# Graph attention: the bend of the leaky slope moved from ScalarE to GpSimd

## The chip, the cores and the metric

The kernel runs on one core of one Trainium2 chip. The metric is the device time of one execution in microseconds (us). The engines are named as in the profile: PE (TensorE matmul), PEld (TensorE weight load), DVE (VectorE), ACT (ScalarE), POOL (GpSimd), SP (SyncE, which starts most DMAs).

## The reference, cut to what matters

The whole network has four graph layers and four feed-forward layers over 625 nodes and 10000 edges. The change touches only the first graph layer, a graph attention with 8 heads:

```python
score = s_src + s_dst + einsum(diff, a_dif) + einsum(abs(diff), a_abs) + einsum(hr_src * hr_dst, a_prd)
alpha = jax.nn.leaky_relu(score, negative_slope=0.2)
m = segment_max(alpha.T, src)
ex = exp(alpha.T - m[src])
att = ex / (segment_sum(ex, src)[src] + 1e-16)
out = segment_sum(att * h_e[:, dst], src)
```

## The kernel before

The layer is computed densely: for a tile t of 125 source nodes and a head h there is a score for each of the 625 target nodes, a tile of 125 x 625 float32. There are 5 tiles (NT) and 8 heads (HEADS0), so 40 heads k = 8 t + h in one pipeline. A term u of the source node (the tile U, one number for each partition, tile and head) is left out of the raw score x and comes back in the biases. The leaky slope is split: leaky(x+u) = 0.2 (x+u) + 0.8 relu(x+u), and the exponential is taken of the two parts apart and multiplied. For one head k the engines do the following, each in its own written-out order, tied by semaphores:

- PE `raw(k)`: six matmuls into RAW in PSUM (L923, L925), after `raw_taken` of head k-1.
- DVE `raw_scores(k)`: RAW plus the gathered pair scores TSC into SP0[k % 4], with the row maximum (L2125; its second input TSC lies in SBUF with a stride of 8 elements; counts up raw_taken).
- ACT `bent(k)`: BENT[k % 4] = relu(SP0 + U), 125 x 625 (L1455; bent_ready).
- DVE `shift(k)`: two tiny instructions on SH, 125 x 2 and 125 x 1 (L2134, L2136; negmax_ready), the biases of the two exponentials. L2134 has two SBUF inputs beside its scalar, SLOPES and UP.
- ACT `exp_scores(k)`: two exponentials of 125 x 625, SP0 with scale 0.2 (L1461; slope_ready) and BENT with scale 0.8 (L1462; bend_ready).
- POOL `counted(k)`: SP0 times the edge counts CNT (L1744; counted_ready).
- DVE `weighted(k)`: SP0 times BENT with the row sum (L2144; both inputs in SBUF; weights_summed).
- PE `turn_head(k)`: five transposes (L935); ACT `turned_head(k)`: their copy (L1466); PE: ten matmuls with the values HE (L957).

In iteration k of the loop DVE runs `left` (every fourth head, L2105), raw_scores(k+4), weighted(k+2), shift(k+4), `add_heads` at h == 2 of the next tile (L2152 to L2160 and the norm statistics, L1863 to L1866, L1871), and every third head one group of the weight quantization of the next layer (`quantized`, L2114 and L2115, 128 x 512). ACT runs exp_scores(k+3), turned_head(k+1), bent(k+4), `left` (L1447) and its part of the quantization (L1416, L1417, L1428). POOL runs counted(k+3), an inverse root (L1700) once a tile and `signed`, its part of the quantization (L1738, 128 x 512). SP starts the loads of the pair scores of tile t+1 (L568) when a tile's raw scores have been taken.

Of the kernel before, what the change touches and what calls it, by code (L numbers as in the profile page):

```python
# [19 lines left out]
ALU, ACT, AX = mybir.AluOpType, mybir.ActivationFunctionType, mybir.AxisListType  # L20

N, E, D = 625, 10000, 512
P, NT = 125, 5
# [5 lines left out]
HEADS0, DH0 = 8, 64  # L29
# [3 lines left out]
NEG = -1.0e30  # L33
# [178 lines left out]
def program(nc, a, out, loops):  # L212
# [3 lines left out]
    def sb(name, shape, dt=F32):  # L216
        return ctx.enter_context(nc.sbuf_tensor(name, shape, dt))
# [15 lines left out]
    with ctx:  # L233
# [51 lines left out]
        TS = sb("TS", [128, SCORES_AHEAD, HEADS0])  # L285
        CW = sb("CW", [128, ET, 2])
        NODE = sb("NODE", [P, 2, NT])
        U = sb("U", [P, NT, HEADS0])
        UP = sb("UP", [P, NT, HEADS0, 2])
        SH = sb("SH", [P, 2, HEADS0, 2])  # L290
        SLOPES = sb("SLOPES", [P, 2])
# [23 lines left out]
        def view(at, parts, *shape, dt=F32):  # L315
# [69 lines left out]
        BENT = [view(PT_ + 12250, P, N), BENT_SPARE[:, :]] + [  # L385
            MASK_FLAT[:, 1250 * b:1250 * (b + 1)].bitcast(F32) for b in range(2)]
        SP0 = [view(HT_ + 625 * b, P, N) for b in range(4)]
# [67 lines left out]
        scaled_ready, raw_filled, raw_taken = sem("scaled_ready"), sem("raw_filled"), sem("raw_taken")  # L455
        bent_ready, slope_ready, bend_ready = sem("bent_ready"), sem("slope_ready"), sem("bend_ready")
        counted_ready = sem("counted_ready")
        heads_turned, heads_taken = sem("heads_turned"), sem("heads_taken")
        negmax_ready, exp_ready, sums_ready = sem("negmax_ready"), sem("exp_ready"), sem("sums_ready")
        weights_summed, prob_ready = sem("weights_summed"), sem("prob_ready")  # L460
# [818 lines left out]
        def _(act):  # L1279
            n = Tally("act")  # L1280
            psum = Slots(slots, n)
            fn = nc.scalar.activation
# [39 lines left out]
            s, k, _ = psum.next("N")  # L1322
# [5 lines left out]
            for t in range(NT):  # L1328
                s = take("N")
                fn(HR[0:P, t, :, 0, :], s.ap[0:P, :].rearrange("p (h d) -> p h d", d=DH0), ACT.Copy)  # L1330
                fn(Y[0:P, t, :], s.ap[0:P, :], ACT.Copy).then_inc(s.taken, 1)
            for t in range(NT):
                s = take("N")
                fn(HE[:, t, :], s.ap[0:P, :], ACT.Copy).then_inc(s.taken, 1)
            psum.skip(T=ET // 4, W=STEPS + 1)
            s = take("N")
            fn(U[:, :, :], s.ap[0:P, 0:8 * NT].rearrange("p (t h) -> p t h", t=NT), ACT.Copy)\
                .then_inc(s.taken, 1)
            s = take("N")
            fn(PRODUCT[:, :], s.ap[:, 0:HEADS0], ACT.Copy).then_inc(s.taken, 1)  # L1340
# [54 lines left out]
            for t in range(NT):  # L1395
                for rows in (HRT_LOW, HRT_HIGH):
                    s = take("T")
# [49 lines left out]
                fn(LEFT[:, u % 2, 0, :, :], s.ap[:, 0:4 * P].rearrange("p (h n) -> p h n", h=4), ACT.Copy)\  # L1447
                    .then_inc(scaled_ready, 1)

            def bent(k):  # L1450
                t, h = divmod(k, HEADS0)
                act.wait_ge(raw_taken, k + 1)
                if k >= 4:
                    act.wait_ge(weights_summed, k - 3)
                fn(BENT[k % 4], SP0[k % 4], ACT.Relu, bias=U[:, t, h:h + 1]).then_inc(bent_ready, 1)  # L1455

            def exp_scores(k):
                t, h = divmod(k, HEADS0)
                act.wait_ge(negmax_ready, n.add(negmax_ready))
                act.wait_ge(bent_ready, k + 1)  # L1460
                fn(SP0[k % 4], SP0[k % 4], ACT.Exp, bias=SH[:, t % 2, h, 0:1], scale=0.2).then_inc(slope_ready, 1)  # L1461
                fn(BENT[k % 4], BENT[k % 4], ACT.Exp, bias=SH[:, t % 2, h, 1:2], scale=0.8).then_inc(bend_ready, 1)  # L1462
# [5 lines left out]
            HEADS_ALL = NT * HEADS0  # L1468
            left(0)
            left(1)  # L1470
            for k in range(4):
                bent(k)
                if k:
                    exp_scores(k - 1)
            act.wait_ge(uv_ready, 3)
            ahead = quantized(0, late=True)
            turned_head(0)
            for k in range(HEADS_ALL):
                if k + 3 < HEADS_ALL:
                    exp_scores(k + 3)  # L1480
                if k + 1 < HEADS_ALL:
                    turned_head(k + 1)
                if k + 4 < HEADS_ALL:
                    bent(k + 4)
                if k % 4 == 2:
                    left((k + 6) // 4)
                if k == 2 or (k % 3 == 0 and k):
                    next(ahead, None)
# [192 lines left out]
        def _(pool):  # L1681
# [52 lines left out]
            def signed(u):  # L1734
                for k, (j, c, width) in enumerate(groups_of(u)):
# [3 lines left out]
                     .then_inc(quant_ready, 1)  # L1739
                    yield  # L1740

            def counted(k):
                pool.wait_ge(slope_ready, k + 1)
                g.tensor_tensor(SP0[k % 4], SP0[k % 4], CNT[:, k // HEADS0, :], ALU.mult).then_inc(counted_ready, 1)  # L1744

            pool.wait_ge(sums_merged, NT)
            ahead = signed(0)
            for k in range(3):
                counted(k)
            for k in range(NT * HEADS0):  # L1750
                t, h = divmod(k, HEADS0)
                if k + 3 < NT * HEADS0:
                    counted(k + 3)
                if h == 2 and t:
                    inverse_roots([t - 1])
                if k % 3 == 2 and k >= 5:
                    next(ahead, None)
# [74 lines left out]
        def _(dve):  # L1832
# [10 lines left out]
            def step(ins):  # L1843

                ins.then_inc(vector_step, 1)
                dve.wait_ge(vector_step, n.add(vector_step))
# [239 lines left out]
            v.memset(SLOPES[:, 0:1], -0.2)  # L2086
            v.memset(SLOPES[:, 1:2], -0.8)
            v.memset(UP[:, :, :, 0:1], 0.0)
            step(v.tensor_scalar(UP[:, :, :, 1], U[:, :, :], -0.8, None, ALU.mult))
            for lo in (0, DH0):  # L2090
                rows = slice(lo, lo + DH0)
                v.tensor_tensor(
# [37 lines left out]
            def shift(k):  # L2130
                t, h = divmod(k, HEADS0)
                z = SH[:, t % 2, h, :]
                dve.wait_ge(raw_taken, k + 1)
                step(v.scalar_tensor_tensor(z, SLOPES[:, :], HM[:, t % 2, 0, h:h + 1], UP[:, t, h, :],  # L2134
                                            ALU.mult, ALU.add))
                v.tensor_scalar(z[:, 1:2], z[:, 1:2], 0.0, None, ALU.min).then_inc(negmax_ready, 1)  # L2136
                n.add(negmax_ready)

            def weighted(k):
# [562 lines left out]
```

## Time and profile before

| What | Value |
|---|---|
| median of 3 runs | 2611.85 us (2609.61 to 2612.3) |
| time of the profiled execution | 2604.66 us |
| its span in the profile | 2602.7 us |
| busy share PE / DVE / ACT / POOL | 86% / 42% / 28% / 20% |
| the pipeline of 40 heads | from 478.4 us to about 667 us of the span |

The span is the time from the first to the last instruction in the trace; the execution's own time is 2 us longer. Busy shares are means over the whole network; for the change only the stretch of the 40 heads counts, 7% of the span.

### The profile page before, as it was taken

What the parts mean: (1) busy time and instruction counts of PE and PEld (TensorE: products, weight loads), DVE (VectorE), ACT (ScalarE), POOL (GpSimd) and SP (SyncE); (2) the same over time, 40 slices, a digit from 0 to 9 for tenths busy, and PEclk for the clock granted to TensorE, in tenths of its full rate; (3) what the DMA queues carried; (4) which work ended last, traced back from release to release, by engine and by line L of the source; (5) the groups of instructions that cost most, each with busy time, mean ns of one, the idle gap of its engine ahead of it and who ended that gap; (6) DMA issues with size and microseconds to landing.
All of it is one profiled execution on the core that took longest, in us unless ns stands there. A gap on an engine that the chain in (4) does not pass through costs nothing.

```text
span 2602.7 us, 23114 instructions
## 1 busy us (share of the span) xinstructions
PE 2245.6 (86%) x8032; PEld 1281.9 (49%) x8032; DVE 1090.4 (42%) x2470; ACT 724.8 (28%) x1201; POOL 531.2 (20%) x471
## 2 busy tenths in 40 slices
PE   4789868588889888887898899799899889999998
PEld 2566545467545544444354455345445444444443
DVE  4777665499322432345545335424435340000002
ACT  1066553477321110002133124115115111111111
POOL 1647762244211000000200200110110120012211
PEclk9899888688799978997899899899999979999999
DMA  9322222421120110004100200300211057777752
GB/s 373 75 51 59 41 60 60 112 58 25 49 85 16 49 49 19 0 0 172 49 1 16 103 0 0 114 4 0 72 45 49 0 186 296 298 294 301 303 190 64
DMA packets 61469, 243.15 MB, mean 93 GB/s; under 512 B 23183, under 2 KB 25699, under 8 KB 39244
## 3 DMA queue, kind: packets, MB, share of 16 engines
q1 hardware_dynamic: 30742, 173.98, 18.9%
q0 software_dynamic: 26336, 62.19, 7.8%
q10 hardware_dynamic: 4292, 5.76, 0.6%
q8 instruction: 50, 0.82, 0.1%
q14 instruction: 49, 0.40, 0.1%
HBM read 209.96 MB, written 31.92 MB: 93 GB/s over the span
## 4 chain that ended last, share of the span: by engine, by line
PE 56%; DVE 14%; issue 13%; DMA 7%; ACT 4%; POOL 3%; ACTq 1%; PEldq 0%; PEld 0%; SPq 0%; DVEq 0%; POOLq 0%
PE PS L705 18%; PE PS L712 11%; PE PS L1198 6%; PE PS L1207 6%; PE PS L1236 6%; DMA pair_scores<-TS,SIDX 5%; DVE ST L1863 1%; PE PS L997 1%; POOL pair_scores L1724 1%; DVE AR L2144 1%; PE PS L1216 1%; PE PS L750 1%; DVE Y L1871 1%; DVE Y L2414 1%; DVE Y L2415 1%
## 5 line engine op out<-in xcount | busy, mean ns | idle before, releaser
L705 PE MATMUL PS<-XT,WR 128*128 128x113 f32 (+2 forms) x1264 | 363.5, 448 | 8.1 <-ACT XT L1316 7.6
L1700 POOL TENSOR_TENSOR RSTD<-VE,HALF 125x1 f32<-125x1 f32 x105 | 73.8, 703 | 1161.4 <-DVE VE L1866 1161.4
L705 PEld LDWEIGHTS PS<-XT,WR 128*128 128x128 f32 (+1 forms) x1264 | 199.7, 196 | 180.7 <-issue 178.6
L848 PE MATMUL PS<-HR,HOT 125*125 125x512 f32 x800 | 218.7, 423 | 47.4 <-DVE HOT L2008 47.4
L712 PE MATMUL PS<-WR,XT 128*125 128x512 f32 (+1 forms) x480 | 207.9, 586 | 6.5 <-ACT XT L1628 4.2
L705 PE MATMUL PS<-AR 125*128 125x512 f32 (+3 forms) x680 | 193.4, 439 | 9.9 <-ACT AR L1600 4.4
L2588 DVE TENSOR_TENSOR AR<-AR,PS 128x512 f32<-128x512 f32 (+1 forms) x44 | 30.2, 687 | 405.4 <-PE PS L1207 405.4
L848 PEld LDWEIGHTS PS<-HR,HOT 125*125 125x125 f32 x800 | 152.3, 199 | 90.7 <-DVE HOT L2008 40.7
L1888 DVE TENSOR_TENSOR AR<-PS,AR 125x512 f32<-125x512 f32 x55 | 38.0, 692 | 311.0 <-PE PS L712 310.6
L712 PE MATMUL PS<-WR,AR 128*125 128x512 f32 (+1 forms) x370 | 157.2, 576 | 10.2 <-ACT AR L1633 4.6
L705 PEld LDWEIGHTS PS<-AR 125*128 125x128 f32 (+1 forms) x680 | 105.9, 189 | 98.6 <-issue 89.2
L1713 POOL DMA_INDIRECT pair_sums<-CW,SIDX x80 | 136.4, 1705 | 53.4 <-issue 22.7
L712 PEld LDWEIGHTS PS<-WR,XT 128*125 128x125 f32 x480 | 90.0, 191 | 103.4 <-issue 98.4
L1316 ACT ACTIVATE XT<-PS 128x500 f32<-128x500 f32 x70 | 40.7, 590 | 319.3 <-PE PS L725 318.9
L1724 POOL DMA_INDIRECT pair_scores<-TS,SIDX x80 | 86.8, 1085 | 144.9 <-DMA pair_scores<-TS,SIDX 85.2
L712 PEld LDWEIGHTS PS<-WR,AR 128*125 128x125 f32 x370 | 67.1, 192 | 94.6 <-issue 86.5
L1660 ACT ACTIVATE AR<-PS 128x512 f32<-128x512 f32 (+1 forms) x44 | 26.3, 597 | 300.0 <-PE PS L1198 300.0
L725 PE MATMUL PS<-CS,Y 125*128 125x125 f32 x280 | 59.5, 365 | 51.9 <-DVE Y L1871 30.9
L705 PE MATMUL PS<-CNT,AR 125*128 125x512 f32 (+1 forms) x240 | 72.1, 463 | 21.3 <-DVE AR L2325 13.3
L1236 PE MATMUL PS<-AR,MODW 128*128 128x512 f32 (+1 forms) x192 | 86.4, 593 | 0.7 <-ACT MODW L1649 0.7
L2020 DVE TENSOR_REDUCE TS<-WR 125x8 f32<-125x512 f32 x80 | 54.4, 680 | 66.1 <-DMA pair_scores<-TS,SIDX 66.1
L1744 POOL TENSOR_TENSOR AR<-AR,CNT 125x625 f32<-125x625 f32 x40 | 58.9, 1473 | 100.9 <-ACT AR L1461 100.9
(385 smaller groups left out, 3685.6 us busy)
## 6 DMA issues: line engine op xcount, KB each, us to landing
WR<-in_qkv SPq DMA_DIRECT2D x12, 1024.0 KB
WR<-in_omm SPq DMA_DIRECT2D x12, 1024.0 KB
pair_scores<-CNT SPq DMA_DIRECT2D x1, 12212.0 KB, 58.0
AR<-pair_scores SPq DMA_DIRECT2D x5, 2187.5 KB
AR<-in_x_a SPq DMA_DIRECT2D x10, 1024.0 KB, 9.5
AR<-in_x_b SPq DMA_DIRECT2D x10, 1024.0 KB, 4.8
AR<-in_x_c SPq DMA_DIRECT2D x10, 1024.0 KB, 7.2
WR<-in_x_a SPq DMA_DIRECT2D x8, 1024.0 KB, 9.0
```

What stands on the lines that cost most here:

```text
L705: last = mm(s.ap[0:parts, c0:c1], lhs(k), rhs(k)[:, c0:c1], start=(k == 0), stop=(k == terms - 1))
L712: last = mm(s.ap[0:P, 0:cols], lhs, rhs, start=(k == 0), stop=(k == len(pairs) - 1))
L725: last = nc.tensor.transpose(s.ap[:, P * c:P * (c + 1)], Y[0:P, t, 128 * c:128 * (c + 1)], ID[0:P, 0:P])
L848: last = mm(DIFF[m % 4], HOT[g % 2][0:P, k, tile(j)], HR[0:P, k, :, b, :], start=(k == 0 and b == 0), stop=(k == NT - 1 and b == 1))
L1198: last = mm(bank(2 + k % 2, rows_of(k)), stationary(k, c), w[:, c, :], start=(c == 0), stop=(c == K4 - 1))
L1207: last = mm(bank(4 + k % 2, rows_of(k)), stationary(k, c), w[:, c, :], start=(c == 0), stop=(c == K4 - 1))
L1236: last = mm(bank(6 + n % 2, rows), HTX[k % 2][:, c, 0:rows], w[:, c, :], start=(u == 0 and c == 0), stop=((is_shared(k) or u == 1) and c = ...
L1700: g.tensor_tensor(RSTD[:, t:t + 1], VE[:, t:t + 1], HALF[:, :], ALU.pow)\
L1713: g.indirect_dma_start(out=pair_sums[m % 2], out_offset=bass.IndirectOffsetOnAxis(ap=SIDX[:, m:m + 1], axis=0), in_=CW[:, m, :], in_offset ...
L1724: g.indirect_dma_start(out=pair_scores, out_offset=bass.IndirectOffsetOnAxis(ap=SIDX[:, m:m + 1], axis=0), in_=TS[:, m % SCORES_AHEAD, :], ...
L1744: g.tensor_tensor(SP0[k % 4], SP0[k % 4], CNT[:, k // HEADS0, :], ALU.mult).then_inc(counted_ready, 1)
L2020: v.tensor_reduce(TS[0:P, m % SCORES_AHEAD, :], Z[m % 4].rearrange("p (h d) -> p h d", d=DH0), AX.X, ALU.add).then_inc(score_ready, 1)
```

## The change

The bend is computed as max(min(x, 1e30), -u) on POOL instead of relu(x+u) on ACT. This is relu(x+u) - u, so the part 0.8 u that is missing is put into the bias of the second exponential. ACT now writes the tile MINUS_U (scale -1) where it wrote U, and bent(k) stands in POOL's order ahead of counted(k-1).

```diff
-fn(U[:, :, :], s.ap[0:P, 0:8 * NT].rearrange("p (t h) -> p t h", t=NT), ACT.Copy)\
+fn(MINUS_U[:, :, :], s.ap[0:P, 0:8 * NT].rearrange("p (t h) -> p t h", t=NT), ACT.Copy, scale=-1.0)\
...
             # ACT
-            def bent(k):
-                t, h = divmod(k, HEADS0)
-                act.wait_ge(raw_taken, k + 1)
-                if k >= 4:
-                    act.wait_ge(weights_summed, k - 3)
-                fn(BENT[k % 4], SP0[k % 4], ACT.Relu, bias=U[:, t, h:h + 1]).then_inc(bent_ready, 1)
...
-            for k in range(4):
-                bent(k)
-                if k:
-                    exp_scores(k - 1)
+            for k in range(3):
+                exp_scores(k)
...
-                if k + 4 < HEADS_ALL:
-                    bent(k + 4)
...
             # POOL
+            def bent(k):
+                t, h = divmod(k, HEADS0)
+                pool.wait_ge(raw_taken, k + 1)
+                if k >= 4:
+                    pool.wait_ge(weights_summed, k - 3)
+                g.tensor_scalar(BENT[k % 4], SP0[k % 4], -NEG, MINUS_U[:, t, h:h + 1], ALU.min, ALU.max)\
+                 .then_inc(bent_ready, 1)
...
-            for k in range(3):
-                counted(k)
+            for k in range(4):
+                bent(k)
+                if k:
+                    counted(k - 1)
             for k in range(NT * HEADS0):
                 t, h = divmod(k, HEADS0)
+                if k + 4 < NT * HEADS0:
+                    bent(k + 4)
                 if k + 3 < NT * HEADS0:
                     counted(k + 3)
...
             # DVE
-            step(v.tensor_scalar(UP[:, :, :, 1], U[:, :, :], -0.8, None, ALU.mult))
+            step(v.tensor_scalar(UP[:, :, :, 1], MINUS_U[:, :, :], 0.8, None, ALU.mult))
...
-                v.tensor_scalar(z[:, 1:2], z[:, 1:2], 0.0, None, ALU.min).then_inc(negmax_ready, 1)
+                v.tensor_scalar(z[:, 1:2], z[:, 1:2], 0.0, UP[:, t, h, 1:2], ALU.min, ALU.subtract).then_inc(negmax_ready, 1)
```

## Rows read from the trace of the kernel before

**Rows 1.** The stretch in windows: busy us (x instructions), clock, DMA share, GB/s.
```profile
core 0: us, PE busy (x) PEld busy (x) DVE busy (x) ACT busy (x) POOL busy (x), PEclk, DMA share, GB/s
478.40:491.00 12.60, 6.17 (x18) 4.47 (x18) 7.17 (x17) 6.22 (x9) 3.04 (x2) 0.50 0.56 148
...
520.00:545.00 25.00, 19.03 (x136) 15.79 (x134) 24.52 (x47) 19.90 (x31) 10.70 (x9) 0.99 0.08 15
545.00:558.00 13.00, 11.48 (x61) 10.55 (x62) 9.75 (x22) 8.87 (x14) 4.76 (x4) 0.62 0.77 192
558.00:580.00 22.00, 17.98 (x130) 15.15 (x128) 21.59 (x42) 19.22 (x31) 10.94 (x8) 0.97 0.01 1
580.00:594.00 14.00, 12.37 (x79) 11.01 (x79) 12.15 (x26) 9.66 (x15) 7.36 (x6) 0.80 0.71 179
594.00:615.00 21.00, 15.87 (x113) 13.07 (x112) 20.55 (x41) 16.91 (x26) 9.35 (x8) 1.00 0.01 1
615.00:632.00 17.00, 16.12 (x85) 14.45 (x86) 13.63 (x27) 11.85 (x19) 8.55 (x6) 0.70 0.01 1
632.00:652.80 20.80, 17.66 (x100) 14.60 (x98) 20.39 (x37) 16.00 (x25) 10.00 (x7) 0.84 0.00 1
```
**Rows 2.** Waits, 478 to 663 us: us in total, times, longest.
```profile
POOL AR L1744 <- ACT AR L1461: 100.9, 36, 21.5
...
DVE AR L2125 <- PE PS L925: 23.3, 14, 3.5
```
**Rows 3.** Groups by shape, 440 to 720 us: busy us, mean ns, idle before.
```profile
L1744 POOL TENSOR_TENSOR AR<-AR,CNT 125x625 f32<-125x625 f32 x40 | 58.9, 1473 | 100.9 <-ACT AR L1461 100.9
...
L2125 DVE CUSTOM_DVE_ANT_0 AR<-PS,AR 125x625 f32<-125x625 f32 x40 | 51.7, 1292 | 45.6 <-PE PS L925 23.3 <-DMA AR<-pair_scores 22.1
...
L1461 ACT ACTIVATE AR<-AR,SH 125x625 f32<-125x625 f32 x40 | 32.5, 813 | 11.5 <-DVE SH L2136 10.6
...
L2144 DVE CUSTOM_DVE_ANT_0 AR<-AR,MASK 125x625 f32<-125x625 f32 x20 | 24.5, 1226 | 1.9 <-POOL AR L1744 1.9
...
L2134 DVE SCALAR_TENSOR_TENSOR SH<-SLOPES,HM,UP 125x2 f32<-125x2 f32 x40 | 22.0, 549 | 0.1
...
L1738 POOL TENSOR_TENSOR WR<-WR 128x512 f32<-128x512 f32 x12 | 17.8, 1479 | 3.3 <-DVE WR L2115 3.3
...
L1455 ACT ACTIVATE MASK<-AR,U 125x625 f32<-125x625 f32 x20 | 16.3, 815 | 14.8 <-DVE HM L2125 14.8
...
L2144 DVE CUSTOM_DVE_ANT_0 AR<-AR,BENT_SPARE 125x625 f32<-125x625 f32 x10 | 11.4, 1142 | 0.0
L2144 DVE CUSTOM_DVE_ANT_0 AR<-AR 125x625 f32<-125x625 f32 x10 | 10.9, 1092 | 0.0
```
**Rows 4.** Duration ns min/median/max of L2144 and L2134, then L2114 and L2115.
```profile
L2144 DVE CUSTOM_DVE_ANT_0 AR<-AR,MASK x20: 800/866/2000, 495.7 to 658.0; 125x625 f32<-125x625 f32 x20
...
L2134 DVE SCALAR_TENSOR_TENSOR SH<-SLOPES,HM,UP x40: 208/213/1551, 479.8 to 654.8; 125x2 f32<-125x2 f32 x40
...
L2114 DVE SCALAR_TENSOR_TENSOR WR<-WR x12: 680/682/686, 516.4 to 658.7; 128x512 f32<-128x512 f32 x12
...
L2115 DVE TENSOR_TENSOR WR<-WR x12: 691/692/1662, 517.2 to 659.4; 128x512 f32<-128x512 f32 x12
```
**Rows 5.** DVE and POOL in order of time: start us, us, instruction.
```profile
564.79 1.30 DVE L2125 CUSTOM_DVE_ANT_0 AR<-PS,AR 125x625 f32<-125x625 f32 x1
...
566.01 0.81 DVE L2144 CUSTOM_DVE_ANT_0 AR<-AR,MASK 125x625 f32<-125x625 f32 x1
566.53 1.66 POOL L1744 TENSOR_TENSOR AR<-AR,CNT 125x625 f32<-125x625 f32 x1 [2.70 <-ACT AR L1461]
...
566.74 1.47 DVE L2134 SCALAR_TENSOR_TENSOR SH<-SLOPES,HM,UP 125x2 f32<-125x2 f32 x1
568.25 0.15 DVE L2136 TENSOR_SCALAR SH<-SH 125x1 f32<-125x1 f32 x1
```
**Rows 6.** The last counted head and the weighted head behind it.
```profile
656.17 1.29 POOL L1744 TENSOR_TENSOR AR<-AR,CNT 125x625 f32<-125x625 f32 x1 [1.92 <-ACT AR L1461]
...
657.96 0.81 DVE L2144 CUSTOM_DVE_ANT_0 AR<-AR,MASK 125x625 f32<-125x625 f32 x1 [1.93 <-POOL AR L1744]
```
**Rows 7.** The only POOL instruction that fills 625 float32 a partition.
```profile
L1688 POOL MEMSET EA<- 128x625 f32 x1 | 0.6, 611 | 0.0
```
**Rows 8.** The chain that ended last, 495 to 510 us: start us, us.
```profile
501.94 0.82 ACT BENT_SPARE L1455
502.84 0.82 ACT AR L1461
...
504.84 0.81 ACT MASK L1455
```

More of the change, by code:

```diff
@@ L287, in program @@
         NODE = sb("NODE", [P, 2, NT])
-        U = sb("U", [P, NT, HEADS0])
+        MINUS_U = sb("MINUS_U", [P, NT, HEADS0])
         UP = sb("UP", [P, NT, HEADS0, 2])
```

## The prediction

> **What bounds the kernel now.** I read the views in this order: the windows over the 40 heads, the waits, the groups by shape, then the order of time around a few heads.
>
> The windows [rows 1] fall into two kinds. In 520 to 545, 558 to 580, 594 to 615 and 632 to 652.8 us DVE is busy 24.52, 21.59, 20.55 and 20.39 us: 87.05 of 88.8 us. There DVE sets the pace. Between them (545 to 558, 580 to 594, 615 to 632) the granted clock has fallen to 0.62, 0.80 and 0.70 of full speed, PE is busy nearly throughout, and DVE is idle 3.25, 1.85 and 3.37 us, together 8.5 us. The first 13 us run at 0.50 (1.2 GHz), with DVE at 57%. Of the 40 raw-score instructions (a mean of 1.29 us each [rows 3]) 14 wait for PE, 23.3 us in all [rows 2], most of them among the first nine heads, before 517 us. So about 22 heads lie in stretches where each us on DVE counts, about 9 in slow-clock stretches where idle time can hide some of it, and 9 at the start where PE hides all of it.
>
> ACT is not the bound, and POOL has the most room: counted(k) waits 100.9 us in total for the exponential of ACT [rows 2].
>
> But DVE's busy time holds waits. L2144 takes 0.80 us at its shortest and up to 2.00 us, L2134 0.21 us and up to 1.55 us [rows 4]. Rows 5 show why. weighted starts at 566.01 and takes its 0.81 us; counted on POOL shows up at 566.53 but ends only at 568.19; the tiny 125 x 2 instruction starts at 566.74 and ends at 568.21, with POOL. DVE's instructions with two SBUF inputs and POOL's product exclude each other for their whole length. The raw-score instruction, with one input in PSUM, keeps its 1.29 us in all 40. Over all heads this costs DVE (24.5 + 11.4 + 10.9) - 40 x 0.80 = 14.8 us in L2144 and 22.0 - 40 x 0.213 = 13.5 us in L2134 [rows 3, 4], and 1 us in the one long L2115: 29.3 us, 0.73 us a head.
>
> The Trainium skill says the same of this port (SBUF — State Buffer, "Who interferes with whom"): VectorE with two SBUF inputs contends with any GpSimd instruction that reads SBUF, and the loser blocks fully. The trace agrees for GpSimd's products; for an instruction with one tensor input no row here shows it. By that rule the moved instruction blocks as the product does; without it the sum would lose its first term.
>
> **The change, part by part.**
>
> *Off ACT:* 40 x 0.815 us of L1455 [rows 3], 32.6 us. ACT is busy 16.0 to 19.9 us in the four DVE-bound windows of 20.8 to 25 us [rows 1], so nothing of this lies on the path there. It does at the start, where the chain goes through L1455 twice, at 501.94 and 504.84 us [rows 8]. I count 2.5 us gained for these and their neighbours, between 0 and 5.
>
> *MINUS_U, UP and the bias:* the same instructions as before with another constant or one more operand of one element a partition; L2136 takes 0.15 us [rows 5] and keeps it. Nothing.
>
> *Onto POOL:* 40 instructions of 125 x 625 with one tensor input. No row shows one. From below, a memset of 625 elements takes 0.61 us [rows 7]; from above, the product with two inputs takes 1.47 us on average [rows 3]. Nothing excludes a longer one, but there is no nearer row. I take 1.1 us, a little over the middle, since it reads and does two operations. In rows 5 the small instruction is held 1.47 - 0.21 = 1.26 us by a product that takes about 1.5 us, so a hold is the POOL row less 0.25 us: 0.85 us for the bend, with ends 0.36 and 1.22.
>
> The Trainium skill (GPSIMD Engine Reference, "3.1 Elementwise — side-by-side cycle accounting") gives 1.8 cycles an element at 1.2 GHz as the best of a longer loop body, 0.94 us for 625 elements as an estimate. No run shows it. By it the row would be nearer 1.0 us, the sum some 3 us smaller.
>
> *Where it falls.* bent(k+4) is released by the end of raw_scores(k+4). At that same moment DVE starts weighted(k+2) with two SBUF inputs; POOL needs a semaphore first and comes second, as in rows 5. So, in us from the end of raw_scores: weighted 0 to 0.8, bent 0.8 to 1.7, with shift(k+4) held behind it until 1.7; the next raw scores follow shift and start at about 2.1 instead of 1.2. That is the hold, once a head: 22 x 0.85 = 18.7 us in the DVE-bound stretches. Of 9 x 0.85 = 7.7 us in the slow-clock stretches the idle 8.5 us hides about two thirds: 2.5 us. At the start PE hides it; I add 1 us for bent(3), which delays the first weighted.
>
> *What it moves.* counted(k+3) now stands behind bent(k+4) on POOL. Today it runs when the exponential ends and hits weighted or shift. Then it would run from about 1.9 to 3.4, under the raw scores (2.1 to 3.4), which it does not disturb. The 29.3 us of today go. In their place: in the 11 heads with a quantization group counted meets L2114 or L2115, which today pass almost undisturbed [rows 4], at 1.1 us each, 12 us; the 11 signed products of POOL behind it (1.48 us on average [rows 3]) still meet weighted, 0.8 us each, 9 us; four add_heads, 1 us together. So 22 us come back: -29.3 + 22 = -7.3 us.
>
> *A late counted.* A product that starts at 656.17 lets weighted go at 657.96, 1.8 us later, though its row ends after 1.29 [rows 6]. So counted(k+3), started at 1.9, is seen at 3.7, and weighted(k+3) could have started at 3.4. In that gap bent(k+5) is ready and takes the port first, then weighted, then the waiting counted, and only then shift: about 0.9 us more in such a head. I count it for half of the 14 heads in DVE-bound stretches that have no quantization group: 7 x 0.9 = 6 us.
>
> *What queues behind POOL's new wait:* bent(k+4) waits for raw_taken, and behind it stand counted(k+3), signed and the inverse root. counted was ready earlier, but weighted(k+3) comes after raw_scores(k+5) in DVE's order, so only the lateness above is charged. signed and the root have slack: DVE waits 1.9 us in all for counted [rows 3]. SP's loads of the pair scores start with raw_taken, a little later, in stretches with a DMA share of 0.01 to 0.77; they stay hidden.
>
> *Sum:* 18.7 + 2.5 + 1 - 7.3 + 6 - 2.5 = 18.4 us. Against the profiled execution that is 2604.66 + 18 = 2623 us. It lies 7 us under the median, so the forecast on the median is 2611.85 + 18 = 2630 us.
>
> **The rivals.** (A change of less than 0.2%, 5 us, can't be told from none.)
>
> *A. The heavy case, slower still:* the bend costs 1.22 us of hold and today's collisions don't go, since the order of the port keeps shifting. 31 x 1.22 = 38 us, less 2.5 at the start, some 3 hidden: +33 to +38, about 2648. For it: POOL would hold or want the port 2.6 of about 4.8 us a head. Against it: counted is now tied behind the raw scores' end, and should fall under the next.
>
> *B. Faster:* the move of counted under the raw scores is the larger effect. Its place is the 29.3 us of stalls in L2144 and L2134; if none come back and the bend is as short as the memset, 31 heads pay 0.36 us, 11 us, and ACT gives 2.5: -29.3 + 11 - 2.5 = -21 us, 2591. It decides where the hold of the bend stays under about (29.3 + 2.5) / 31 = 1.0 us and the quantization heads don't collide. For it: the order on POOL really does take counted out of the way. Against it: the two-input groups L2114 and L2115 follow shift exactly when counted starts.
>
> *C. No change to be told:* the bend does not block DVE at all, or is short (0.36 us), with the collisions as in the forecast: 22 x 0.36 = 8, plus 1, -7.3, plus 2 for late counteds, -1.5: +2, 2614. Without any block, counted again starts while weighted and shift run, as today, so the gain is small too: 2607 to 2614.
>
> *D. The clock:* the clock fell to 0.50 after each add_heads stretch; a slower DVE leaves PE more gaps, and more stretches at 1.2 GHz could follow. A head at the slow clock takes 4 to 5 us on PE, not more than the new DVE period, so this adds a few us inside the forecast, not a case of its own.
>
> **How the numbers follow.** Forecast (2617 to 2643, with bends of 0.7 to 1.47 us) 0.47; A 0.18; C 0.15; B 0.20. B is seldom at its full price, so the range reaches down to 2599, leaving out about one in ten below, and up to 2654 for A: one in ten above. The likeliest case's own range is 2617 to 2643. Faster 0.20, same 0.15, slower 0.65.
>
> **What would show each step.** Right: a POOL row TENSOR_SCALAR x40 near 1.1 us; L2134 held in most heads, its mean up from 0.55 us to about 1.0 and more; L2144's mean down from 1.17 us towards 0.9; L2114 or L2115 longer than 0.69 in many of 12; the stretch from the first raw scores to the last 10% longer; ACT idle more. Wrong: L2134 near 0.21 us throughout (no block, or a short one), a bend below 0.7 or above 1.6 us, or weighted waiting long for POOL by semaphore, which would mean that POOL's own 2.6 us in series set the pace.

## The result, and the profile after

The changed kernel takes 2619.88 us (median of 15 runs) against 2612.57 us for the kernel before in 15 runs beside it: a ratio of 1.003, with a 95% interval of 1.0022 to 1.0038. It is slower by 0.3%: 7.3 us between the medians, about 8 us by the ratio, where 18 us were forecast.

The page of the changed kernel, span and busy time:

```profile
span 2617.5 us, 23114 instructions
...
PE 2249.4 (86%) x8032; PEld 1282.7 (49%) x8032; DVE 1104.7 (42%) x2470; ACT 696.6 (27%) x1161; POOL 579.2 (22%) x511
```

VectorE's busy time is 1104.7 us; it was 1090.4 us. Those 14.3 us are where the change shows first. The 40 instructions that left ScalarE are on GpSimd (511 instead of 471).

I measure the stretch of the 40 heads from the start of the first raw scores to the start of the last inverse root: 669.52 - 478.44 = 191.1 us before, 682.87 - 481.88 = 201.0 us after, 9.9 us more. The other 4.9 us of the 14.8 us between the two spans lie outside it: 3.4 us before the first head, whose start lay anywhere from 477.5 to 483.6 us in the fourteen profiled kernels of this study, and 1.5 us behind the stretch. So I use the stretch beside the ratios. It comes from one execution of each kernel, but divided by the time before, its difference lies within the interval of the ratio, or on its edge, in all thirteen kernels.

VectorE in three parts of the stretch, first the kernel before, then the changed one: from the first raw scores to the tenth, from there to the last (30 heads), and behind (us, busy us, granted clock, DMA share, GB/s):

```profile
478.44:517.77 39.33, 23.12 (x53) 0.68 0.32 86
517.77:652.82 135.05, 124.83 (x240) 0.87 0.18 45
652.82:669.52 16.70, 8.06 (x21) 0.53 0.42 163
```

```profile
481.88:520.18 38.30, 27.17 (x54) 0.70 0.36 93
520.18:665.51 145.33, 133.62 (x239) 0.86 0.17 41
665.51:682.87 17.36, 9.51 (x21) 0.52 0.30 115
```

The first part is 1.0 us shorter, the 30 heads are 10.3 us longer, the end is 0.7 us longer. In the 30 heads VectorE is busy 8.8 us more and idle 1.5 us more.

Groups by shape of the changed kernel, 440 to 730 us (busy us, mean ns | idle before), to be read against [rows 3]:

```profile
L1741 POOL TENSOR_TENSOR AR<-AR,CNT 125x625 f32<-125x625 f32 x40 | 57.2, 1430 | 3.1
...
L2135 DVE SCALAR_TENSOR_TENSOR SH<-SLOPES,HM,UP 125x2 f32<-125x2 f32 x40 | 27.0, 676 | 0.1
L1736 POOL TENSOR_SCALAR MASK<-AR,MINUS_U 125x625 f32<-125x625 f32 x20 | 24.5, 1223 | 23.9 <-DVE HM L2126 23.5
...
L2145 DVE CUSTOM_DVE_ANT_0 AR<-AR,MASK 125x625 f32<-125x625 f32 x20 | 19.5, 976 | 3.5 <-POOL AR L1741 3.4
L2115 DVE SCALAR_TENSOR_TENSOR WR<-WR 128x512 f32<-128x512 f32 x12 | 18.9, 1572 | 0.0
...
L2145 DVE CUSTOM_DVE_ANT_0 AR<-AR 125x625 f32<-125x625 f32 x10 | 10.3, 1032 | 0.3 <-POOL AR L1741 0.3
...
L2145 DVE CUSTOM_DVE_ANT_0 AR<-AR,BENT_SPARE 125x625 f32<-125x625 f32 x10 | 9.6, 960 | 0.0
...
L2137 DVE TENSOR_SCALAR SH<-SH,UP 125x1 f32<-125x1 f32 x40 | 8.6, 214 | 1.4
...
L2153 DVE TENSOR_SCALAR HM<-HM 125x8 f32<-125x8 f32 x5 | 5.5, 1103 | 0.0
```

counted (L1741) no longer waits for ScalarE: its idle time before is 3.1 us, since the bend in front of it now does the waiting. weighted (L2145) has become shorter, 39.4 us in all against 46.8. The first instruction of shift (L2135) has become longer, 27.0 us against 22.0. The group instruction L2115 has gone from 682 ns to 1572 ns, and the 125 x 8 one of add_heads (L2153) from 162 ns to 1103 ns.

One head in order of time (start us, us):

```profile
543.05 0.80 DVE L2145 CUSTOM_DVE_ANT_0 AR<-AR 125x625 f32<-125x625 f32 x1
543.23 1.27 POOL L1736 TENSOR_SCALAR MASK<-AR,MINUS_U 125x625 f32<-125x625 f32 x1 [1.48 <-DVE HM L2126]
...
543.78 0.74 DVE L2135 SCALAR_TENSOR_TENSOR SH<-SLOPES,HM,UP 125x2 f32<-125x2 f32 x1
544.55 0.21 DVE L2137 TENSOR_SCALAR SH<-SH,UP 125x1 f32<-125x1 f32 x1
544.59 1.52 POOL L1741 TENSOR_TENSOR AR<-AR,CNT 125x625 f32<-125x625 f32 x1
544.68 1.46 DVE L2153 TENSOR_SCALAR HM<-HM 125x8 f32<-125x8 f32 x1
```

The order is the one forecast: weighted first, the bend behind it, shift held until the bend ends (544.50), then counted, which takes the next instruction of VectorE with it (here L2153). The bend holds shift in this way in 36 of the 40 heads. But the bend's row of 1.27 us begins while weighted still has the port. Only about 0.65 us of it lie behind weighted (ends at 543.85), and shift is held 0.74 - 0.21 = 0.53 us. At the start of the stretch, where nothing competes, the bend's row is short:

```profile
483.36 0.78 POOL L1736 TENSOR_SCALAR AR<-AR,MINUS_U 125x625 f32<-125x625 f32 x1 [16.80 <-DVE HM L2126]
...
486.68 0.82 POOL L1736 TENSOR_SCALAR BENT_SPARE<-AR,MINUS_U 125x625 f32<-125x625 f32 x1 [2.55 <-DVE HM L2126]
```

Where counted went is not quite what was forecast. I compared the last 1.29 us of each of its rows (its shortest length), 51.6 us in all, with what VectorE does in that time. Under weighted there were 12.2 us, now 1.5. Under the raw scores, where the forecast put it, there were 22.0 us, now only 15.5. It has moved to the group (1.9 to 11.2 us), to add_heads (0 to 5.0) and to time in which VectorE is idle (4.4 to 12.9).

### The profile page after: what moved, and what is told of

Same layout as the page of the kernel before. It is cut to its first block, busy times and chain, and to the rows that moved or that the text cites. A ratio compares the mean times of both kernels' runs of the same rounds, so it can differ in the third digit from the quotient of the medians.

```text
span 2617.5 us, 23114 instructions
## 1 busy us (share of the span) xinstructions
PE 2249.4 (86%) x8032; PEld 1282.7 (49%) x8032; DVE 1104.7 (42%) x2470; ACT 696.6 (27%) x1161; POOL 579.2 (22%) x511
## 4 chain that ended last, share of the span: by engine, by line
PE 56%; issue 13%; DVE 12%; DMA 7%; POOL 5%; ACT 4%; ACTq 1%; PEldq 0%; PEld 0%; SPq 0%; DVEq 0%; POOLq 0%
PE PS L705 18%; PE PS L712 11%; PE PS L1198 6%; PE PS L1207 6%; PE PS L1236 6%; DMA pair_scores<-TS,SIDX 5%; PE PS L848 2%; POOL AR L1741 1%; DVE ST L1864 1%; PE PS L997 1%; PE PS L1216 1%; PE PS L750 1%; DVE Y L1872 1%; DVE Y L2415 1%; DVE Y L2416 1%
## 5 line engine op out<-in xcount | busy, mean ns | idle before, releaser
L1649 ACT ACTIVATE AR<-PS 128x512 f32<-128x512 f32 (+1 forms) x44 | 26.3, 597 | 300.1 <-PE PS L1198 300.1
L725 PE MATMUL PS<-CS,Y 125*128 125x125 f32 x280 | 58.1, 360 | 51.9 <-DVE Y L1872 30.7
L725 PEld LDWEIGHTS PS<-CS,Y 125*128 125x128 f32 x280 | 42.6, 186 | 70.5 <-issue 38.3
```

The source lines that it names most:

```text
L725: last = nc.tensor.transpose(s.ap[:, P * c:P * (c + 1)], Y[0:P, t, 128 * c:128 * (c + 1)], ID[0:P, 0:P])
```

## The experiments

The table sums up, for each kernel, the time that VectorE's instructions spent beyond their unhindered length. It is worked out from the groups by shape as in the prediction: busy time less the count times 0.213 us for shift's first instruction of two columns (0.220 in its form with one input), 0.80 for weighted, 0.682 and 0.691 for the group, 0.162 for the 125 x 8 of add_heads.

| kernel | shift held | weighted held | group held | add_heads held | sum us | stretch us | ratio to before (95%) |
|---|---|---|---|---|---|---|---|
| before | 13.5 | 14.8 | 1.0 | 0 | 29.3 | 191.1 | 1 |
| the change | 18.5 | 7.4 | 10.7 | 4.7 | 41.3 | 201.0 | 1.003 (1.0022 to 1.0038) |
| bias_operand_alone | 12.5 | 17.1 | 1.0 | 0 | 30.6 | 190.5 | 0.9991 (0.998 to 1.0002) |
| shift_one_input | 0 | 9.4 | 11.8 | 1.0 | 22.2 | 192.1 | 1.0005 (0.9994 to 1.0017) |
| bend_write_only | 43.2 | 2.2 | 0 | 0 | 45.4 | 195.4 | 1.0017 (1.0007 to 1.0028) |
| counted_before_bend | 18.7 | 19.2 | 1.0 | 0 | 38.9 | 198.1 | 1.0025 (1.0012 to 1.0037) |
| before_shift_two_columns | 12.5 | 17.2 | 1.0 | 0 | 30.7 | 190.5 | 1.0005 (0.9994 to 1.0016) |
| before_shift_one_column | 0 | 12.8 | 6.0 | 1.9 | 20.7 | 183.8 | 0.9973 (0.9961 to 0.9986) |
| no_bend | 8.5 | 16.6 | 1.2 | 0 | 26.3 | 187.4 | 0.999 (0.9981 to 0.9999) |
| write_only_one_input | 0 | 5.1 | 8.6 | 3.7 | 17.4 | 179.7 | 0.9957 (0.994 to 0.9973) |
| no_bend_one_column | 0 | 18.0 | 5.0 | 0 | 23.0 | 186.4 | 0.9979 (0.9969 to 0.9988) |
| counted_first_one_input | 0 | 12.6 | 7.8 | 2.0 | 22.4 | 188.3 | 0.9984 (0.9975 to 0.9994) |
| one_column_and_tie | 0 | 3.9 | 7.9 | 3.6 | 15.4 | 182.4 | 0.9967 (0.9956 to 0.9977) |
| tie_alone | 41.2 | 1.2 | 0 | 0 | 42.4 | 195.4 | 1.0026 (1.0016 to 1.0037) |

### The longer bias instruction

```diff
-v.tensor_scalar(z[:, 1:2], z[:, 1:2], 0.0, None, ALU.min)
+v.tensor_scalar(z[:, 1:2], z[:, 1:2], 0.0, UP[:, t, h, 0:1], ALU.min, ALU.subtract)
```

> The kernel before, with only the tiny bias instruction (L2136) given a fourth operand of one column (a column of zeros, so the output stays the same). The bend stays on ScalarE. If the longer bias instruction is a part of the loss, it takes 0.21 us in place of 0.15 in all 40 heads, 2.4 us on VectorE, and the time is up by 1 to 2.5 us (ratio 1.0004 to 1.001). The rival, that one more small operand costs nothing on the path, gives 1.000.

The instruction takes 214 ns in place of 154 ns in all 40 heads, but the ratio is 0.9991 with 1 inside the interval, and the stretch is 0.6 us shorter. The part is not a cause that can be seen.

### Shift with one input

```diff
-step(v.scalar_tensor_tensor(z, SLOPES[:, :], HM[:, t % 2, 0, h:h + 1], UP[:, t, h, :], ALU.mult, ALU.add))
-v.tensor_scalar(z[:, 1:2], z[:, 1:2], 0.0, UP[:, t, h, 1:2], ALU.min, ALU.subtract)
+top = HM[:, t % 2, 0, h:h + 1]
+step(v.tensor_scalar(z[:, 0:1], top, -0.2, None, ALU.mult))
+v.tensor_scalar(z[:, 1:2], top, MINUS_U[:, t, h:h + 1], -0.8, ALU.max, ALU.mult)
```

> The changed kernel, with shift computed by two VectorE instructions of one tensor input each: -0.2 times the row maximum, and -0.8 times max(row maximum, -u). No instruction of shift has two SBUF inputs any more. Theory (the bend's hold of the port in front of shift is a main part of the loss): the 18.5 us that L2135 spent beyond its own 0.21 us go, the chain of two steps is 0.1 us shorter, VectorE's busy time falls by 15 to 25 us, and the time by 8 to 16 us against the changed kernel, so a ratio of 0.997 to 1.000 to the kernel before. Rival 1 (small instructions with one input are held by GpSimd too, as the 125 x 8 one in add_heads was, 1.22 us in the median): ratio 1.002 to 1.004, as the change itself. Rival 2 (GpSimd's serial pair, bend and counts, sets the pace by its semaphores): the time VectorE gains comes back as waits of weighted for counted; ratio 1.001 to 1.003.

The minimum, median and maximum of both instructions of shift (ns):

```profile
L2136 DVE TENSOR_SCALAR SH<-HM x40: 141/146/158, 484.9 to 660.3; 125x1 f32<-125x1 f32 x40
L2137 DVE TENSOR_SCALAR SH<-HM,MINUS_U x40: 212/214/215, 485.1 to 660.5; 125x1 f32<-125x1 f32 x40
```

Neither is ever held, though the bend runs beside them. Most of the loss is gone: the stretch is 8.9 us shorter than with the change, and the ratio is 1.0005. The ratio came just above the range of the theory, and below those of both rivals. The edit changes two things at once, the number of inputs and the number of columns, and spares VectorE some time of its own; which of them counts is taken up below. Not all of the gain stayed: the group's second instruction, which the change left alone, now meets counted, 1516 ns on average against 692.

```profile
L2116 DVE TENSOR_TENSOR WR<-WR 128x512 f32<-128x512 f32 x12 | 18.2, 1516 | 0.4
```

And VectorE waits 9.1 us in all for GpSimd's product and ScalarE's exponential ahead of weighted, where it waited 3.7 us with the change.

### The bend left out, GpSimd only writes

```diff
-g.tensor_scalar(BENT[k % 4], SP0[k % 4], -NEG, MINUS_U[:, t, h:h + 1], ALU.min, ALU.max)
+g.memset(BENT[k % 4], 0.0)
```

> The changed kernel with the bend left out: GpSimd fills BENT with zeros (a memset of 125 x 625 in place of the bend), so that the second exponential is taken of the bias alone. Everything else and all waits stay. Theory (the port is held by GpSimd's reading): the memset, 0.6 us, holds nothing; the first instruction of shift goes back to 0.21 us in all heads, VectorE loses the 18.5 us, the ratio to the kernel before is 0.996 to 1.000. Rival (any GpSimd instruction that starts under weighted holds shift until it ends): shift is held 0.2 to 0.4 us a head still, ratio 1.001 to 1.003.

The theory failed. The ratio of 1.0017 lies in the rival's range, but not by the rival's mechanism: it had shift held 0.2 to 0.4 us a head by the memset, and shift is held 1.1 us, by counted. In order of time:

```profile
563.56 0.81 DVE L2144 CUSTOM_DVE_ANT_0 AR<-AR 125x625 f32<-125x625 f32 x1
563.71 0.62 POOL L1736 MEMSET MASK<- 125x625 f32 x1 [3.00 <-DVE HM L2125]
564.28 1.29 POOL L1740 TENSOR_TENSOR AR<-AR,CNT 125x625 f32<-125x625 f32 x1
...
564.29 1.30 DVE L2134 SCALAR_TENSOR_TENSOR SH<-SLOPES,HM,UP 125x2 f32<-125x2 f32 x1
```

The memset takes its 0.62 us while weighted runs; it holds nothing and is held by nothing. But it ends before weighted does, so that counted behind it already asks for the port when weighted gives it up, and gets it ahead of shift. shift is then held for the whole product: 43.2 us over all heads, more than behind the real bend. The bend had stood between shift and counted, and shift passed in the gap between the two.

### The other order on GpSimd

```diff
-if k + 4 < NT * HEADS0: bent(k + 4)
 if k + 3 < NT * HEADS0: counted(k + 3)
+if k + 4 < NT * HEADS0: bent(k + 4)
```

> The changed kernel with the two GpSimd instructions of an iteration swapped: counted(k+3), then bent(k+4). Theory (two things cost: the bend's hold, and the meeting of counted with the quantization group and add_heads): counted is free to start when its exponential ends, before the raw scores end, and again meets weighted as in the kernel before (stalls of 1.1 us in some 15 heads), while the bend then comes later and meets shift or the group: VectorE's stalls rise from 44 us to 50 to 60, ratio 1.004 to 1.009. Rival (the order on GpSimd tied counted to the raw scores for nothing, and its lateness is what costs): the swap gives back most of the loss, ratio 0.999 to 1.002.

The theory's mechanism is there: weighted is held 19.2 us again and the group hardly. Its price was wrong, for the sum of the holds did not rise. The ratio of 1.0025 lies below its range and above the rival's, and can't be told from the change's own (the stretch is 2.9 us shorter). The order chooses who is held, and matters little as long as shift can be held.

### Shift in the kernel before, two columns and one column

```diff
 # before_shift_two_columns
+step(v.tensor_scalar(z, SLOPES[:, :], HM[:, t % 2, 0, h:h + 1], None, ALU.mult))
+v.tensor_scalar(z[:, 1:2], z[:, 1:2], UP[:, t, h, 1:2], 0.0, ALU.add, ALU.min)
 # before_shift_one_column
+v.tensor_scalar(z[:, 0:1], top, -0.2, None, ALU.mult)
+step(v.tensor_scalar(z[:, 1:2], top, -0.8, UP[:, t, h, 1:2], ALU.mult, ALU.add))
+v.tensor_scalar(z[:, 1:2], z[:, 1:2], 0.0, None, ALU.min)
```

> The kernel before (bend on ScalarE), with the first instruction of shift reading one tensor only: SLOPES (125 x 2) times the row maximum; -0.8 u is added in the second, 125 x 1. Two instructions as before. Theory (two SBUF inputs are what holds an instruction behind counted): the 13.5 us of L2134 go, the stretch of the 40 heads is 5 to 10 us shorter than 191 us, ratio 0.996 to 0.998. Rival (an instruction with one input of an even number of columns is held as well, as the 125 x 8 one in add_heads was in the changed kernel): the first instruction keeps its mean near 0.5 us, ratio 0.999 to 1.001.

> The kernel before, with shift as three VectorE instructions of 125 x 1 and one input each (-0.2 times the maximum; -0.8 times the maximum less 0.8 u; the minimum with zero). One instruction more than before, 0.15 us. Theory (these were never held in the run of the changed kernel with the one-input shift): 13.5 us of holding go, 40 x 0.15 = 6 us come, net 7 us less on VectorE, of which some show up again as weighted held by counted: ratio 0.997 to 0.9995. Rival: the port is so full that a hold taken from shift comes back in weighted in full, ratio 1.000 to 1.003.

The first instruction with two columns (first row), and the two that take its place with one column (ns, minimum, median, maximum):

```profile
L2134 DVE TENSOR_SCALAR SH<-SLOPES,HM x40: 215/220/1525, 481.4 to 656.0; 125x2 f32<-125x2 f32 x40
```

```profile
L2135 DVE TENSOR_SCALAR SH<-HM x40: 137/144/158, 484.8 to 652.6; 125x1 f32<-125x1 f32 x40
L2136 DVE TENSOR_SCALAR SH<-HM,UP x40: 193/198/215, 484.8 to 652.7; 125x1 f32<-125x1 f32 x40
```

The rival won the first: an instruction with one tensor input but two columns is held up to 1.5 us, and the time is that of before. With one column none of the instructions is held, and one instruction more gives a faster kernel: 0.9973, 7.3 us less in the stretch. The name of the earlier run, one input, says too little; it is the single column.

The Trainium skill (VectorE: DVE Perf Modes, "Mode 2×_2P — use both read ports for one tensor") says that a single-input instruction may stream two halves over both ports when its outermost dimension that is not one is even, or odd and the same in source and destination. The trace agrees with that as the reason why 125 x 2 and 125 x 8 are held and 125 x 1 is not; no run here shows the halves themselves, no odd number of columns above one was tried, and no single column with two tensor inputs.

### The bend on no engine

```diff
-fn(BENT[k % 4], SP0[k % 4], ACT.Relu, bias=U[:, t, h:h + 1])
-fn(SP0[k % 4], SP0[k % 4], ACT.Exp, bias=SH[:, t % 2, h, 0:1], scale=0.2)
-fn(BENT[k % 4], BENT[k % 4], ACT.Exp, bias=SH[:, t % 2, h, 1:2], scale=0.8)
+fn(BENT[k % 4], SP0[k % 4], ACT.Exp, bias=SH[:, t % 2, h, 0:1], scale=0.2)
+fn(SP0[k % 4], SP0[k % 4], ACT.Exp, bias=SH[:, t % 2, h, 1:2], scale=0.8)
```

> The kernel before with the bend left out: ScalarE takes both exponentials of the raw score (slope into BENT, bend part in place in SP0), and no engine computes a minimum or maximum. It tells what taking the bend off ScalarE is worth when nothing is put on GpSimd. My prediction counted 2.5 us for that: the stretch of the 40 heads 186 to 191 us (before 191.1), ratio 0.998 to 1.000. Rival (ScalarE is worth nothing here, or its later exponentials were good for the order on the port): 191 us or more, ratio 1.000 to 1.002.

> The kernel before with the bend left out altogether and shift in three instructions of one column. The floor: no bend on any engine, no hold of shift. Before with the three-instruction shift took 183.8 us for the 40 heads and without the bend 187.4 us instead of 191.1. If the two gains add, 180 us and a ratio of 0.996; if ScalarE's relief only counts while shift is held, 183 us and 0.997.

Relief of ScalarE is worth 3.7 us of stretch, where I had counted 2.5 us. All of it lies where the prediction put it, at the start: the tenth raw scores begin 34.8 us after the first, where before they begin 39.3 us after them, and what follows is 0.9 us longer. Together with the one-column shift the two gains did not add: 186.4 us, not 180, and no better than the one-column shift with the bend still on ScalarE (183.8). Again 4.3 us are gained up to the tenth raw scores, and 6.9 us are lost behind them. With ScalarE free the exponentials come earlier, and so counted, which then meets weighted: 18.0 us of holds there against 12.8.

### What the bend's reading costs once shift is safe

The same memset in the kernel with the one-input shift, and the same swap of order:

> The changed kernel with both edits: the one-input shift, and the bend left out (GpSimd fills BENT with zeros, a memset). Nothing of the bend reads through the port now, and shift can't be held. Against the run with the one-input shift and the real bend (stretch of the 40 heads 192.1 us) only the bend's reading is gone. Theory (once shift is safe, the bend still costs because it fills the port and pushes counted later, onto the quantization group and weighted): the stretch is 182 to 187 us, ratio 0.995 to 0.998. Rival (it is the tie of counted to the end of the raw scores, which the memset keeps): 190 to 193 us, ratio 0.999 to 1.001.

> The changed kernel with the one-input shift and with counted(k+3) ahead of bent(k+4) on GpSimd. The bend stays on GpSimd. Theory (the port's load is what is left; the order only chooses who is held): the stretch stays within 2 us of 192.1, ratio 0.999 to 1.002. Rival (the tie of counted to the raw scores is what the bend's place costs): the stretch falls to 186 to 189 us, ratio 0.997 to 0.999.

The groups of weighted, and of the memset, in write_only_one_input:

```profile
L2144 DVE CUSTOM_DVE_ANT_0 AR<-AR,MASK 125x625 f32<-125x625 f32 x20 | 18.9, 944 | 2.7 <-POOL AR L1740 2.7
...
L1736 POOL MEMSET MASK<- 125x625 f32 x20 | 12.5, 623 | 28.2 <-DVE HM L2125 28.2
```

Replacing the bend by a write of the same size, with every wait kept, shortens the stretch from 192.1 to 179.7 us: 12.4 us, more than the theory had asked for. Of these, 4.8 us are holds (22.2 to 17.4) and 6.4 us waits of VectorE for counted or the exponentials (9.1 to 2.7); the memset's row is 0.62 us instead of 1.24. The memset differs from the bend in two ways, it does not read and it is 0.2 us shorter than an unhindered bend, so the 12.4 us are the price of both. The swap gave 3.8 us: 188.3 us and 0.9984 lie in the ranges of the rival, and the theory is refuted. The tie of counted to the raw scores, behind the bend, does cost something. The holds stay as they were (22.4 us against 22.2), but VectorE's waits for counted or the exponentials fall from 9.1 to 2.9 us. Of the two, taking the bend's work out gives three times as much.

### What the change got right, put into the kernel before

The memset run, with its stretch of 179.7 us, suggests that the tie of counted to the next head's raw scores is useful where no bend stands in between. So it was put into the kernel before, with the bend left on ScalarE:

```diff
 def counted(k):
+    pool.wait_ge(raw_taken, min(k + 2, NT * HEADS0))
     pool.wait_ge(slope_ready, k + 1)
```

> The kernel before (bend on ScalarE, all of the computation kept), with shift in three instructions of one column, and with counted(k) on GpSimd made to wait for raw_taken of head k+1, as it does behind the bend in the changed kernel. Theory (what the change got right is that tie, which puts counted behind weighted and under the raw scores; what it got wrong is the bend's reading through the port): 179 to 182 us for the 40 heads, as in the run with the memset (179.7), against 183.8 without the tie and 191.1 before; ratio 0.9945 to 0.997. Rival (the short run with the memset was short because ScalarE had no bend, and the tie does nothing): 183 to 185 us, ratio 0.997 to 0.998. Second rival (ScalarE with the bend gives its exponentials late, and tied counteds come later still): 186 us or more.

> The kernel before with the tie alone: counted(k) waits for raw_taken of head k+1; shift keeps its instruction with two SBUF inputs. Theory (counted, released with weighted, comes directly behind it and takes the port ahead of shift, as behind the memset): the first instruction of shift is held about 1.1 us in nearly every head, 45 to 50 us in all, and weighted hardly at all; the stretch takes 194 to 197 us (the run with the memset and this shift took 195.4), ratio 1.001 to 1.003. Rival (the tie helps whatever shift does): below 190 us, ratio 0.999 or less.

The first instruction of shift in tie_alone, then weighted and the group in one_column_and_tie:

```profile
L2135 DVE SCALAR_TENSOR_TENSOR SH<-SLOPES,HM,UP 125x2 f32<-125x2 f32 x40 | 49.7, 1242 | 0.1
```

```profile
L2146 DVE CUSTOM_DVE_ANT_0 AR<-AR,MASK 125x625 f32<-125x625 f32 x20 | 18.9, 944 | 2.2 <-POOL AR L1745 2.2
L2115 DVE SCALAR_TENSOR_TENSOR WR<-WR 128x512 f32<-128x512 f32 x12 | 16.1, 1340 | 0.0
...
L2146 DVE CUSTOM_DVE_ANT_0 AR<-AR 125x625 f32<-125x625 f32 x10 | 9.0, 905 | 0.0
```

tie_alone came as forecast in time, with 41.2 us of holds in shift, a little under the forecast, and 1.2 us in weighted. With the one-column shift the same wait cuts weighted's holds from 12.8 to 3.9 us; 3.6 of these 8.9 us come back in the group and add_heads. The kernel is faster than the kernel before and than tie_alone, 0.9967 with 0.9956 to 0.9977; but its stretch of 182.4 us is only 1.4 us under the one with the one-column shift and no tie, and just outside the theory's range, and the ratios of these two can't be told apart. Behind the tenth raw scores it takes 143.0 us, as the memset run does (142.9; without the tie 144.5). The 2.7 us between this kernel and the memset run are gained before (36.8 against 39.4 us), where the memset run has no bend on ScalarE: for that part the first rival was right. The single-column shift is the gain that is sure.

## Why the prediction was right and wrong

**Right: the direction and the mechanism.** The bend does hold VectorE through the shared port, in the place that the prediction named, in nearly every head: the median of L2135 is 732 ns in place of 213, and it is held in 36 of 40 heads. counted has moved behind the bend and away from weighted, as said, though less than before of it lies under the raw scores (15.5 us, 22.0 before).

**The step that failed** is the size of the first term: "I take 1.1 us, a little over the middle", and from it a hold of 0.85 us a head. Unhindered the bend takes 0.78 to 0.82 us, and the hold is 0.52 us. The rule of the row less 0.25 us holds for this unhindered length, 0.8 - 0.25 = 0.55, and not for the row beside weighted, 1.23 us on average, which begins with a wait. The estimate of 0.94 us from the Trainium skill (GPSIMD Engine Reference, "3.1 Elementwise — side-by-side cycle accounting") was nearer than my own value, and still above the 0.8 us measured. Put into the prediction's own sum, 0.52 us gives 22 x 0.52 = 11.4, a third of 9 x 0.52 = 1.6, then 1 - 7.3 + 6 - 2.5: 10.2 us, against 9.9 us in the stretch. Most of that closeness is luck, for three other terms were wrong and cancel: the late counted, what idle time hides, and the bias.

**What came back.** I had 22 us of collisions returning in place of today's 29.3. Without those of shift, the trace has 7.4 us in weighted, 10.7 us in the group and 4.7 us in add_heads, 22.8 us. All the places were named. The signed products were priced at 9 us and hold weighted for 5.8 of its 7.4 us; add_heads was priced at 1 us, since I had looked only at its instruction with two inputs; the one that is held is the 125 x 8 one with a single input.

**The late counted,** 6 us in the sum, is hardly there: weighted waits 3.7 us for counted by semaphore where it waited 1.9, and of the 3.7 us only 0.8 lie in the 30 heads. That a shorter bend lets counted start sooner would explain it; no run tests this.

**The bias instruction** was priced at nothing. On VectorE it costs 40 x 0.06 = 2.4 us; alone it moves no time.

**What idle time hides.** The prediction let the idle time in the slow-clock stretches hide two thirds of nine holds, 5.2 us. It hid nothing that can be seen. VectorE's waits for PE did fall, from 23.3 to 19.2 us, but all of that lies before the tenth raw scores (15.7 to 10.6 us), where the first part is 1.0 us shorter; behind them they rose from 7.6 to 8.6 us.

**The start.** ScalarE's relief was to give 2.5 us there, and the bend to take 1 us. The relief alone gives 4.6 us (no_bend), and the change keeps 1.0 us of it.

**The balance.** VectorE's busy time: shift 18.5 - 13.5 = +5.0, weighted 7.4 - 14.8 = -7.4, group 10.7 - 1.0 = +9.7, add_heads +4.7, bias +2.4, together +14.4 us; the page shows 14.3. Its idle time in the stretch fell by 4.4 us, 5.1 less before the tenth raw scores, 1.5 more in the 30 heads and 0.8 less behind them. 14.3 - 4.4 = 9.9 us. The prediction's sum with measured terms is 30 x 0.52 = 15.6 for the hold, -29.3 + 22.8 = -6.5 for the collisions, 0.8 for the late counted, 30 x 0.06 = 1.8 for the bias and -1.0 for the start: 10.7 us.

**The rivals.** A, the heavy case, did not occur: in the 30 heads VectorE waits only 0.8 us for GpSimd's products, so GpSimd's time in series is no new pace. B had two conditions. A hold under 1.0 us came true with 0.52, but the quantization heads did collide, 10.7 us. write_only_one_input, 0.9957, shows that a gain lies there, but only with no reading and a shift that can't be held. C had the bend not block, or hold 0.36 us a head: it does block, but with 0.52 us it lies nearer to C's short bend than to the forecast's 0.85, and so does the time. D was not seen: the granted clock is 0.80 over the stretch in both kernels, 0.87 and 0.86 in the 30 heads.

**Signs.** L2134's mean was to rise to 1.0 us or more and rose to 0.68. L2144's was to fall towards 0.9 and fell to 0.985. L2114 was to be longer than 0.69 us and is 1.57. The bend's row was to be near 1.1 us and is 1.23; this sign misleads, since a row released beside weighted holds a wait, 0.62 us of 1.27 in the head shown. The stretch was to be 10% longer and is 5% longer.

**What stays open.** The experiments separate the bend's reading from the rest, not the hold of shift alone in the changed kernel: shift_one_input also spares VectorE one longer instruction. A second bend in each head, which would give the slope of time over reading, was not tried. Each stretch comes from one execution; kernels that hardly differ from the kernel before (bias_operand_alone, before_shift_two_columns) lie 0.6 us from it, so differences of 1 us or so show nothing.

## What to carry to other kernels

Before work goes to GpSimd, list what VectorE runs within the next microsecond with two SBUF inputs, or with one and more than one column (2 and 8 columns were held here): each such instruction, however tiny, can be held for the whole GpSimd instruction. Here the instruction of 125 x 2 numbers took up to 1.5 us, and splitting it into single columns in the kernel before won about as much (0.27%) as the offload lost (0.3%). And where two engines share a port, the order of requests decides who pays; removing one request can hand the port to a longer one, so look at who asks next.

## What the runs showed of the hardware that was not expected

- A VectorE instruction of 125 x 1 with one tensor input was never held (137 to 158 ns in 40 in before_shift_one_column), one of 125 x 2 with one input was (215 to 1525 ns in before_shift_two_columns), and so was one of 125 x 8 (165 to 1455 ns in the changed kernel).
- GpSimd's memset of 125 x 625 takes 0.62 us beside weighted and holds nothing; the minimum and maximum of the same size with one tensor input takes 0.78 to 0.82 us unhindered and 1.27 us when released beside weighted. A GpSimd row holds its wait for the port; what it costs VectorE is the part behind the other's end.
